# Decoder layer on one core: the first stage reordered, three pieces of its work moved between engines

## The reference

```python
def _L0_attn_ref(x):                      # 16 heads of 16
    Q, K, V = (proj(W) for W in (q_proj, k_proj, v_proj))
    scores = einsum('bhqd,bhkd->bhqk', Q, K) / sqrt(16)
    attn = softmax(where(causal, -inf, scores))
    return (attn @ V) @ o_proj.T
def _L0_xattn_ref(x, token_ids):          # expert e = min(id // 3125, 3), weights from ctx_2048
    return silu(x @ Wg[e].T) * (x @ Wu[e].T) @ Wd[e].T
def _L0_ffn_ref(x):                       # expert = argmax of softmax(x @ Wr + br)
    return (silu(x @ Wg[e]) * (x @ Wu[e])) @ Wd[e] * top_probability
x = layernorm(x + _L0_attn_ref(x))
x = layernorm(x + _L0_xattn_ref(x, ids))
x = layernorm(x + _L0_ffn_ref(x))
```

## Time and profile before

| | |
|---|---|
| median of 3 runs | 294.6 us (292.76 to 295.98) |
| the profiled execution | 293.57 us |
| its span, first to last instruction | 291.8 us |
| busy: PE, PEld | 234.3, 189.1 us |
| busy: DVE, ACT, POOL | 191.7, 135.3, 66.1 us |
| mean granted TensorE clock | 0.939 |

### The profile page before, as it was taken

One profiled execution on the slowest core, in us unless ns is written; L12 is line 12 of the kernel. 1 busy time (PEld: TensorE's weight loads), 2 busy tenths in 40 slices (PEclk: granted clock), 3 DMA queues, 4 the chain that ended last, 5 costly groups with the idle time before them and its releaser, 6 DMA issues.

```text
span 291.8 us, 7077 instructions
## 1 busy us (share of the span) xinstructions
PE 234.3 (80%) x2714; PEld 189.1 (65%) x2730; DVE 191.7 (66%) x425; ACT 135.3 (46%) x229; POOL 66.1 (23%) x128
## 2 busy tenths in 40 slices
PE   4568678988899897599997346898778999999970
PEld 4356355665676664367796222598768999999960
DVE  4887648786699685569988452789535555556550
ACT  4536355766694885256555151488131333333300
POOL 8500000100020444212122556000113212222222
PEclk9999779999999999789999558999999999999996
DMA  6999244142024444602409412340000000000000
GB/s 189 340 315 318 74 144 152 67 147 72 3 85 135 109 115 177 163 2 72 147 20 403 161 59 81 94 111 2 0 20 20 4 13 20 21 20 20 7 5 15
DMA packets 17424, 28.63 MB, mean 98 GB/s; under 512 B 2733, under 2 KB 12974, under 8 KB 17392
## 3 DMA queue, kind: packets, MB, share of 16 engines
q1 hardware_dynamic: 16048, 25.28, 27.5%
q0 software_dynamic: 1344, 2.90, 2.8%
HBM read 19.43 MB, written 9.50 MB: 99 GB/s over the span
## 4 chain that ended last, share of the span: by engine, by line
PE 56%; DVE 21%; issue 9%; ACT 5%; POOL 4%; DMA 3%; SPq 1%; POOLq 0%; DVEq 0%; ACTq 0%
PE ps L1285 9%; PE ps L1678 7%; PE ps L1679 7%; PE ps L1680 7%; PE ps L1695 3%; PE ps L1697 3%; PE ps L1696 3%; DVE wf_lo L795 3%; PE ps L1362 3%; POOL sorted L519 2%; DVE arena L961 2%; PE ps L1614 2%; DMA ring<-wqkvT 2%; PE ps L1358 2%; ACT wf_hi L559 1%
## 5 line engine op out<-in xcount | busy, mean ns | idle before, releaser
L1678 PE MATMUL ps<-arena,wf_hi 128*128 128x128 f16 x352 | 60.2, 219 | 0.3 <-DVE arena L1197 0.3
L1679 PE MATMUL ps<-arena,wf_hi 128*128 128x128 f16 x352 | 60.3, 218 | 0.0
L1680 PE MATMUL ps<-arena,wf_lo 128*128 128x128 f16 x352 | 60.2, 217 | 0.0
L1679 PEld LDWEIGHTS ps<-arena,wf_hi 128*128 x352 | 34.3, 98 | 0.2
L1678 PEld LDWEIGHTS ps<-arena,wf_hi 128*128 x352 | 33.7, 96 | 0.9 <-issue 0.8
L1680 PEld LDWEIGHTS ps<-arena,wf_lo 128*128 x352 | 33.9, 96 | 0.0
L1695 PE MATMUL ps<-wf_hi,arena 128*128 x88 | 24.0, 273 | 5.9 <-DVE arena L1222 3.4
L795 DVE SCALAR_TENSOR_TENSOR wf_lo<-ring,wf_hi 128x1024 f16<-128x1024 f32 x17 | 20.6, 1219 | 11.0 <-ACT wf_hi L559 5.9
L751 ACT ACTIVATE arena<-ps 128x512 f32<-128x512 f32 x22 | 13.1, 594 | 29.7 <-PE ps L1680 29.7
L1697 PE MATMUL ps<-wf_hi,arena 128*128 x88 | 24.0, 273 | 0.0
L1696 PE MATMUL ps<-wf_lo,arena 128*128 x88 | 24.0, 273 | 0.0
(11 more groups left out here) (223 smaller groups left out, 562.8 us busy)
## 6 DMA issues: line engine op xcount, KB each, us to landing
ring<-Wf SPq DMA_DIRECT2D x17, 512.0 KB, 3.7
sorted<-fill SPq DMA_DIRECT2D x1, 4515.0 KB, 20.8
arena<-Wf SPq DMA_DIRECT2D x7, 512.0 KB, 8.1
arena<-sorted SPq DMA_DIRECT2D x20, 129.0 KB, 2.3
sorted<-fill SPq DMA_DIRECT2D x1, 1161.0 KB, 6.3
ring<-xT SPq DMA_DIRECT2D x4, 256.0 KB, 5.1
X<-x_tok SPq DMA_DIRECT2D x1, 1024.0 KB, 7.8
ring<-ctxT SPq DMA_DIRECT2D x2, 512.0 KB, 3.6
```

Of the source, the lines that this page charges most:

```text
L1678: t.matmul(dst, hi, a_hi[p][:, k], start=k == 0, stop=False)
L1679: t.matmul(dst, hi, a_lo[p][:, k], start=False, stop=False)
L1680: last = t.matmul(dst, lo, a_hi[p][:, k], start=False, stop=k == NK - 1)
```

## The change

- The nine expert numbers are read by one call that loads them all, without the check of each value, in front of the first step; the four loads in front of the fifth tile's projection are gone.
- The products of tiles 0 and 1 go by weight half (`with_high`, `with_low`): both operands' products with the first high half, then with its low half, then the same for the second half. Tile 2's Q and K come before the transposes of tiles 0 and 1. The first scores wait for tile 0's stacks alone, the transposed ones for the buffers they write. The warm-up has 24 products instead of 30.
- GpSimd clears buffer 0 of `QT`, ahead of its clears of buffers 2 and 1, and makes low x of batches 2 and 3, after its other constants.
- `max_rows(0)` is issued in halves, by SP and by ScalarE; ScalarE waits for the transpose in front of `proj_hi(2 * TB)` and has made the output weights' high part by then.
- On VectorE `counts` comes before the low weight halves, `slots` and `pick` come after `maxima(1, 0)`.

```diff
-WARM_START, WARM_GAP = 30, 8
+WARM_START, WARM_GAP = 24, 8
@@ SP
-                for k in range(4):
-                    sp.dma_start(rows[:, k], mT[b % 2][32 * k:32 * (k + 1), :]).then_inc(m_row, 16)
+                for k in range(2 if b == 0 else 4):
+                    sp.dma_start(max_row(b)[:, k], mT[b % 2][32 * k:32 * (k + 1), :]).then_inc(m_row, 16)
@@ GpSimd
             pool.wait_ge(const_m, 2)
+            link(g.memset(QT[0][SLOT:P, 0::2, :].bitcast(F32), 0.0))
+            g.memset(QT[0][0:SLOT, 1::2, :].bitcast(F32), 0.0).then_inc(const_z, 1)
+            pool.wait_ge(const_z, 1)
             link(g.memset(QT[2][SLOT:P, 0::2, :].bitcast(F32), 0.0))
...
+            for b in range(2, B):
+                pool.wait_ge(x_hi, b + 1)
+                pool.wait_ge(x_lo, b)
+                t = slice(b * S, (b + 1) * S)
+                g.tensor_tensor(xTv_lo[:, :, t], xT_st[:, :, t], xTv_hi[:, :, t], ALU.subtract).then_inc(x_lo, 1)
@@ ScalarE
             q_odds(2)
+            act.wait_ge(in_wo, 16)
+            a.activation(wo_hi, wo_st, ACT.Copy, scale=W_SCALE).then_inc(w_hi, 1)
+            act.wait_ge(mT_done, 1)
+            act.wait_ge(const_z, 1)
+            act.wait_ge(const_q2, 2)
+            for k in range(2, 4):
+                a.dma_start(max_row(0)[:, k], mT[0][32 * k:32 * (k + 1), :]).then_inc(m_half, 16)
             proj_hi(2 * TB)
             q_odds(3)
-            act.wait_ge(in_wo, 16)
-            a.activation(wo_hi, wo_st, ACT.Copy, scale=W_SCALE).then_inc(w_hi, 1)
@@ VectorE
-            link(v.tensor_tensor(pick[:, :, :], ge[:, 0:E, NA:NT], ge[:, 1:E + 1, NA:NT], ALU.subtract))
-            v.tensor_scalar(pick[:, :, :], pick[:, :, :], 1 / W_SCALE, None, ALU.mult).then_inc(pick_rdy, 1)
             x_low(0)
+            counts()
             for k in range(NK):
                 dve.wait_ge(w_hi, k + 1)
                 v.scalar_tensor_tensor(out=wqkv_lo[:, k], in0=wqkv_st[:, k], scalar=W_SCALE, in1=wqkv_hi[:, k],
                                        op0=ALU.mult, op1=ALU.subtract).then_inc(w_lo, 1)
-            counts()
-            v.memset(QT[0][SLOT:P, 0::2, :].bitcast(F32), 0.0)
-            v.memset(QT[0][0:SLOT, 1::2, :].bitcast(F32), 0.0).then_inc(const_z, 1)
             x_low(1)
             dve.wait_ge(cnt_sb, 1)
             running()
             slot_tiles(0, NA)
-            slots()
...
             max_T(0)
-            x_low(2)
             proj_lo(3)
             stacks(2)
             proj_lo(2 * TB)
             stacks(3)
-            x_low(3)
             maxima(1, 0)
+            link(v.tensor_tensor(pick[:, :, :], ge[:, 0:E, NA:NT], ge[:, 1:E + 1, NA:NT], ALU.subtract))
+            v.tensor_scalar(pick[:, :, :], pick[:, :, :], 1 / W_SCALE, None, ALU.mult).then_inc(pick_rdy, 1)
+            slots()
@@ TensorE, scores
-                    pe.wait_ge(kT_done, TB * (b + 1))
-                    pe.wait_ge(q_even, TB * (b + 1))
-                    pe.wait_ge(q_odd, TB * (b + 1))
+                    first = 1 if b == 0 else TB * (b + 1)
+                    pe.wait_ge(kT_done, first)
+                    pe.wait_ge(q_even, first)
+                    pe.wait_ge(q_odd, first)
...
+                    if bank == 1 and n == 0:
+                        pe.wait_ge(kT_done, TB)
+                        pe.wait_ge(q_even, TB)
+                        pe.wait_ge(q_odd, TB)
@@ TensorE, scores_T
                 if g == 0:
-                    pe.wait_ge(m_row, 64 * (b + 1))
+                    pe.wait_ge(m_row, rows_in(b))
+                    if b == 0:
+                        pe.wait_ge(m_half, 32)
...
+                    if n == 0:
+                        if bank == 4:
+                            pe.wait_ge(q_even, 3)
+                            pe.wait_ge(q_odd, 3)
+                        else:
+                            pe.wait_ge(kT_done, 3 if bank == 3 else 4)
@@ TensorE, order
             pe.wait_ge(x_lo, 1)
-            pe.wait_ge(w_lo, NK)
-            qkv(0)
+            pe.wait_ge(w_hi, 1)
+            with_high(0, 0)
             pe.wait_ge(cnt_sb, 1)
-            qkv(1)
+            with_high(1, 0)
+            pe.wait_ge(w_lo, 1)
+            with_low(0, 0)
+            with_low(1, 0)
+            pe.wait_ge(w_hi, 2)
+            with_high(0, 1)
+            pe.wait_ge(w_lo, 2)
+            with_low(0, 1)
+            with_high(1, 1)
+            with_low(1, 1)
+            pe.wait_ge(x_lo, 2)
+            qk_product(2)
             stack_T(0)
             stack_T(1)
+            value_product(2)
             pe.wait_ge(const_m, 1)
+            pe.wait_ge(const_z, 1)
             scores(0, 0)
-            pe.wait_ge(x_lo, 2)
-            qkv(2)
+            qkv(3)
             scores(0, 1)
-            qkv(3)
+            stack_T(2)
             scores(0, 2)
-            stack_T(2)
             scores(0, 3)
-            pe.wait_ge(tile_rdy, 1)
-            expert_numbers(4)
             pe.wait_ge(x_lo, 3)
             pe.wait_ge(maxed, 2 * NG - 1)
             qkv(2 * TB)
             stack_T(3)
-            expert_numbers(NSA)
+            pe.wait_ge(tile_rdy, 1)
+            _, experts = nc.values_load_multi_w_load_instructions(
+                tile_i[0:1, 0, 0:NSA], engines=[pe.engine], min_val=0, max_val=E - 1,
+                skip_runtime_bounds_check_because="each is a sum of E - 1 comparisons made on the chip, 0 or 1 each")
```

More of the change, by code:

```diff
@@ L225, in build @@
         kT_rdy, qT_rdy, kT_done, q_even, q_odd = (sem(n) for n in ("kT_rdy", "qT_rdy", "kT_done", "q_even", "q_odd"))
-        s_rdy, maxed, mT_done, m_row = (sem(n) for n in (
-            "s_rdy", "maxed", "mT_done", "m_row"))
+        s_rdy, maxed, mT_done, m_row, m_half = (sem(n) for n in (
+            "s_rdy", "maxed", "mT_done", "m_row", "m_half"))
         st_rdy, exped, av_rdy, o_sb, oS_rdy, o_norm = (sem(n) for n in (
@@ L336, in staged, with max_row, rows_in @@
             return ring[:, r * CH:(r + 1) * CH], in_ch[r], 16 * (n // RING + 1)
+        def max_row(b):
+            return QT[b % 3][3 * DK:3 * DK + 1, :, :].rearrange("o h (t k r) -> o k (h t) r", t=TB, r=32)
+        def rows_in(b):
+            return 64 * (b + 1) - 32
         block = ctx.enter_context(nc.Block())
@@ L381, in max_rows @@
                     sp.wait_ge(const_q2, 2)
-                row = 3 * DK
-                rows = QT[b % 3][row:row + 1, :, :].rearrange("o h (t k r) -> o k (h t) r", t=TB, r=32)
-                for k in range(4):
-                    sp.dma_start(rows[:, k], mT[b % 2][32 * k:32 * (k + 1), :]).then_inc(m_row, 16)
+                for k in range(2 if b == 0 else 4):
+                    sp.dma_start(max_row(b)[:, k], mT[b % 2][32 * k:32 * (k + 1), :]).then_inc(m_row, 16)
             max_rows(0)
@@ L968, in max_T @@
                 if b >= 2:
-                    dve.wait_ge(m_row, 64 * (b - 1))
+                    dve.wait_ge(m_row, rows_in(b - 2))
+                    dve.wait_ge(m_half, 32)
                 v.transpose(mT[b % 2], Mn[b % 2]).then_inc(mT_done, 1)
@@ L1295, in _, with qk_product @@
             count(7, 0, NA)
-            def qkv(tt):
+            def qk_product(tt):
                 tok = slice(tt * P, (tt + 1) * P)
@@ L1302, in qkv, with outputs_of, with_high, with_low @@
                       lambda k: wqkv_lo[:, k, 0:2 * D], NK).then_inc(proj_qk, 1)
+            def qkv(tt):
+                qk_product(tt)
                 if tt < NT - 1:
                     value_product(tt)
+            def outputs_of(tt):
+                return ((ps[:, bank_qk(tt), :], slice(0, 2 * D), proj_qk),
+                        (ps[:, bank_v(tt), 0:D], slice(2 * D, 3 * D), proj_v))
+            def with_high(tt, k):
+                tok = slice(tt * P, (tt + 1) * P)
+                for dst, cols, _ in outputs_of(tt):
+                    t.matmul(dst, xTv_hi[:, k, tok], wqkv_hi[:, k, cols], start=k == 0, stop=False)
+                    t.matmul(dst, xTv_lo[:, k, tok], wqkv_hi[:, k, cols], start=False, stop=False)
+            def with_low(tt, k):
+                tok = slice(tt * P, (tt + 1) * P)
+                for dst, cols, done in outputs_of(tt):
+                    last = t.matmul(dst, xTv_hi[:, k, tok], wqkv_lo[:, k, cols], start=False, stop=k == NK - 1)
+                    if k == NK - 1:
+                        last.then_inc(done, 1)
             def value_product(tt):
@@ L1476, in _ @@
                     pe.wait_ge(const_q2, 2)
-                    for e in (kT_done, q_even, q_odd):
-                        pe.wait_ge(e, 2 * TB)
                 if step != 1:
```

## The result

The change made the kernel slower, by 1.5%: the median is 297.48 us (295.51 to 301.61, 10 runs) against 294.09 for the kernel before on the same chip (292.20 to 295.98, 10 runs), a ratio of 1.0147 (95% interval 1.0111 to 1.0182). Medians are over all executions; the ratios leave out those in the chip's slower state, so the two need not agree. The forecast was 292.7, and the time lies above the range. The profiled execution took 298.62, its span is 296.7, its mean granted clock 0.917 (before 291.8 and 0.939).

A forecast was written before the change was run, and what follows sets the result against it. The prediction took TensorE's queue, blocked by expert-number loads before T0, as the bound. T0 3.6 us earlier less 1.7 later on VectorE gave 1.9 us: 291.7 profiled, 292.7 median; range 288.5 to 295.6, the forecast's own 291.5 to 293.9.

The forecast's parts named there:

- What is late next: Row transfers before attention: SP's rows stand behind the scratch fill and land with it at 34.4, 0.5 us after its last packets.
- T0: Start of the first transposed scores, from which attention runs as one chain; forecast 34.9 against 38.47, 3.6 us earlier.
- the term for the fill's end: Scratch fill on the DMA engines: main part ends near 32.8 instead of 31.0, last engine near 34.0 instead of 32.2.
- The third rival: Slower fill holds the rows longer than the number loads did; T0 from 36.8 on, time 296.3 if unchanged; chance 0.13.
- The clock does not enter: TensorE at T0: granted clock is 0.50 after either pause today, and TensorE will start from a longer pause the same way.
- The transpose of the maxima: Before the row transfers: done near 24.3, where the issues that follow it begin at 29.96 today, 5.6 us earlier.
- GpSimd's clears: Two clears of Q delay the fill's source row 2.0 us; fill issued about 13.4, DMA engines empty 1.8 us.
- The subtractions on GpSimd: Low x of later batches, before the projections: even 2 us each is over before 22.9, when the fifth tile wants it.
- The pick and the slots: VectorE after batch 1's first maxima, in attention: the moved work makes the time 1.7 us later (1.5 to 2.1).
- the second rival: The term for pick and slots on VectorE in attention is not paid; time 291.0; chance 0.12.
- The number load: TensorE before attention: one load of nine values costs 0.65 to 5.9 us, low end taken, hidden by the row transfers.
- ScalarE's rows may pass the fill: Row transfers: ScalarE's two may pass the fill, SP's two not; splitting saves 1.4 us of issue, nothing of T0.

The follow-up runs named there:

- fill_first: Changed kernel with GpSimd preparing the fill's source row before its six clears, so the fill is issued at 8.38; ratio 1.0043 to the kernel before, median 294.28 us.
- fill_late: Changed kernel with SP issuing the scratch fill behind the first row transfers and first weight chunks, at 35.76; ratio 1.0327 to the kernel before.
- slots_in_wait: Changed kernel with VectorE running pick and slots ahead of batch 1's first maxima, while it waits; ratio 1.0121 to the kernel before.
- two_fixes: Changed kernel with first weight chunks waiting for all rows, and pick and slots ahead of batch 1's first maxima; ratio 1.0015 to the kernel before.
- loads_after_rows: Changed kernel with SP waiting for all four rows to land before the first weight chunk; ratio 1.0031 to the kernel before, median 294.06 us.
- after_again: The changed kernel run once more, unedited, for a second profile; median 299.17 us, ratio 1.0132 to the kernel before.
- rows_by_scalar: Changed kernel with all four of batch 0's row transfers issued by ScalarE, none by SP; ratio 1.0145 to the kernel before.
- one_load_early: Changed kernel with one 512 KB weight chunk issued right behind the rows, the others held until the rows land; one time taken, 297.97 us.
- warm_wait: Changed kernel with 42 products into a free bank on TensorE between the last projection and T0; ratio 1.0066 to the kernel before.
- fill_split: Changed kernel with the 4.5 MB fill issued behind the last rows, at 87.30, and pick and slots in VectorE's wait; ratio 0.9926 to the kernel before.

## Why the prediction was wrong

*The step that failed is "What is late next".* Its mechanism held: SP's rows stand behind the fill and land with it. By the counts of their semaphores in the traces they are in 0.3 to 0.5 us behind the fill's end in all eight profiles in which they are queued there (38.39 and 38.04 in the changed kernel). fill_first and fill_late move the fill and T0 moves along. What was mis-sized is the term for the fill's end. The forecast put the rows' landing at 34.4 and T0 at 34.9; they are 38.39 and 38.96, and these 4.1 us are most of the 6.9 by which the profiled time missed (298.62 against 291.7). With the chunks held back the landing is 35.02 and T0 35.6, inside the forecast's bounds. The forecast followed every moved instruction on its own engine, and left out whom low x on GpSimd releases: SP's first two ring loads, which go out 7 us earlier than in the kernel before, into the fill's tail. Their cost was put at nothing. It named a later ring load as having spare time; that a load can do harm by being early it did not ask. The third rival had the outcome (T0 past 36.8, time above 296), through a slower fill as it said; its price of 296.3 was nearer than the forecast.

How the chunks' 3.4 us come about is only partly shown. That holding them back gains about that much is seen twice: 1.0147 against 1.0031, and with the slots in the pause 1.0121 (slots_in_wait) against 1.0015 (two_fixes), intervals apart both times. But by the slices from 14 to 26, before any chunk, the changed kernel's transfers had moved 3,334 KB and those of loads_after_rows 3,771; the missing 437 KB are 1.4 us at that run's 314 GB/s. after_again and slots_in_wait have the same lag (3,399 and 3,356), rows_by_scalar, two_fixes, one_load_early and warm_wait have not (3,724 to 3,882), though nothing in their programs differs in that stretch that the trace shows. So of the 3.3 us by which the fill landed later in the profile, 1.4 were lost ahead of the chunks, and 1.9 are left for them. Their price varies: against the 20.9 us of loads_after_rows, the lag taken off, the fill is longer by 1.9 to 2.2 in the three profiles with the lag, by 0.9 in rows_by_scalar and by 0.5 in warm_wait.

*The clock.* "The clock does not enter" was wrong. Behind T0 it is little: by the mean of its slices (0.83 from 42 to 43, before 0.88 from 41 to 42) it is back at full speed 3.4 us behind T0 instead of 2.8, and the second reduction starts 3.8 us behind T0 instead of 3.5. That is 0.3 us. In the third layer it is more. TensorE waits 2.4 us for VectorE in front of the first down product there, in both kernels (timelines of PE, after and before):

```profile
209.15 0.28 PE L1746 MATMUL ps<-wf_hi,arena 128*128 x1 [2.44 <-DVE wf_lo L813]
```

```profile
205.93 0.28 PE L1695 MATMUL ps<-wf_hi,arena 128*128 x1 [2.44 <-DVE wf_lo L795]
```

With that wait the clock falls in the one and not in the other (windows, after and before):

```profile
211.00:213.00 2.00, 2.00 (x12) 1.38 (x11) 0.00 (x0) 0.00 (x0) 0.00 (x0) 0.50 0.00 0
```

```profile
206.00:208.00 2.00, 2.00 (x19) 1.80 (x20) 0.36 (x1) 0.00 (x0) 0.00 (x0) 1.00 0.00 0
```

In eight profiles of the fourteen it falls, at the end of the wait or within 1 us of it, and the third layer takes 98.0 to 98.3 us at a mean granted clock of 0.98; in the other six it stays at 1.00, and the layer takes 96.6. The stretch between the last maxima and the third layer goes the same way: 92.8 us at a mean of 0.87 before, 93.6 at 0.84 after, 91.0 at 0.91 in loads_after_rows. The executions of the changed kernel differ alike: spans of 293.6 and 294.1 at 0.938, 298.0 at 0.910. At 0.938 it is about 2 us above the 291.8 that the kernel before took at 0.939, which T0's 0.5 and the slots' 1.65 would account for. Why the clock falls at the same wait in one execution and not in another is not shown.

*What came as forecast.* The transpose of the maxima: 4.2 us earlier than the issues of the kernel before, not 5.6: the stacks end at 16.0, not 14.9, and the scores that its last reduction waits for only at 24.29. GpSimd's clears: the fill issued at 13.37, and a slice (13 to 14) in which the DMA engines move nothing; by the shares from 12 to 15 (0.51, 0.01, 0.68) they stand empty for some 1.8 us. The subtractions on GpSimd: 1.16 us each, hidden. The pick and the slots: 1.65 us, all on the chain (two_fixes against loads_after_rows), so the second rival falls. The number load: one instruction of 1.90 us from 26.6 on, nearer to the low end of 0.65 than to 5.9, and hidden as said.

*The rest of the miss*, 6.9 less 4.1 and 0.3, is the third layer's other length (1.7) and the 0.8 between the last maxima and the third layer. Both go with the granted clock.

*The rule from the Trainium skill.* The prediction drew from the Trainium skill, "DMA: Bandwidth & Descriptors", section "Queues, rings and completion order", that ScalarE's rows may pass the fill. They did, but late: by the count of their semaphore they were in at 34.92, 3.1 us ahead of the fill's end, and 0.2 to 3.1 ahead of it in the eight profiles with two rows on each queue. They took 7.9 us (median), 7.2 when ScalarE issued all four, and 1.8 with no fill ahead, and T0 waits for SP's two all the same. The Trainium skill's other section, "Issuing engines are not separate DMA queues", says that issuing from a second engine saves only issue time; the slow landings from ScalarE's queue agree, while T0 of rows_by_scalar does not decide it, its maxima being late.

*Open*: why the rate halves while the DMA share stays full, why three profiles lag from 14 to 26, why SP's first row issue takes 1.85 to 3.59 us, what of the chunks' price is the fill's and what is the rows', whether all rows on ScalarE's queue would bring T0 forward, and why the clock falls at a pause in one execution and not in another.

## What to carry to other kernels

Before you move work earlier, ask what the small transfers at its end will find in front of them in the DMA engines, and which large transfers the same move sets free behind them: a load that goes out early can be the one that makes the chain late. A bulk transfer that is needed late belongs in parts into the stretches where nothing urgent follows it; moved as a whole it only moves the stall (fill_late), or delays the next small transfers (fill_split). Work that is put on an engine in a stretch on the chain belongs into that engine's wait, and where a wait is long the gain from shortening what lies before it is none.

## What the runs showed of the hardware that I had not expected

- 2 KB transfers issued by a second engine took 6.9 to 9.0 us (medians of nine profiles) while the other queue held the fill, and 1.8 us in the three without.
- The fill's tail had slices of 149 to 204 GB/s with two chunks of 512 KB behind it in five profiles (197 to 298 in warm_wait), and of 281 to 326 without, at the same DMA share of about 1.1.
- The first issue of a 2 KB transfer on SP took 1.85 to 3.59 us in seven profiles with the fill queued from 13.4 on, but 0.62 in fill_first with the fill queued from 8.38 on; with no fill queued two took 1.34.
- Nine register values by one load took 1.90 us, 0.21 each; the single loads of before took 0.30, and 0.65 with what surrounds them.
- Where TensorE's pause was filled the clock stayed at full speed past T0, and fell 6.4 us later, after TensorE had stood still from 43 to 44.
- At one and the same wait of 2.4 us the clock fell to 0.50 in eight profiles and stayed at 1.00 in six; the fall made the third layer 1.4 to 1.7 us longer.
